# One more step of a scan's input products on GpSimd, and SiLU of z and the low rows of B and C in other slots

## The reference

```python
xz = x @ in_proj_w.T;  u, z = xz[..., :512], xz[..., 512:]
u = silu(causal_depthwise_conv4(u) + conv_b)
dt_lo, B, C = split(u @ x_proj_w.T, (64, 16, 16))
delta = softplus(dt_lo @ dt_proj_w.T + dt_proj_b);  A = -exp(A_log)
for t:                                   # 2048 positions
    h = exp(delta[t] * A) * h + (delta[t] * u[t]) * B[t]     # 512 x 16 states
    y[t] = h @ C[t]
y = (y + u * D_param) * silu(z)
x = layernorm(x + y @ out_proj_w.T)
h = silu(x @ w1 * s1) * (x @ w2 * s2)
h = gelu(h @ h1 * sh1);  h = gelu(h @ h2 * sh2)
x = layernorm(x + h @ w3 * s3)
```

## Time and profile before

| | us |
|---|---|
| median of 3 runs | 3013.3 (3012.48 to 3014.08) |
| the profiled execution | 3011.42 |
| its span, first to last instruction | 3009.6 |
| VectorE busy in the span | 2297.7 |
| ScalarE busy in the span | 2033.7 |
| GpSimd busy in the span | 1704.2 |
| TensorE matmuls busy in the span | 2720.0 |

### The profile page before, as it was taken

The page is one execution under the profiler, slowest core; times in us unless marked ns, Lnnn a source line. Parts: engine busy times, 40 slices in busy tenths (PEclk is TensorE's granted clock), DMA queues, the critical chain, the costliest instruction groups (busy, mean ns, idle before and its releaser), DMA issues. The chain is left out here.

```text
span 3009.6 us, 40984 instructions
## 1 busy us (share of the span) xinstructions
PE 2720.0 (90%) x11540; PEld 1619.3 (54%) x11540; DVE 2297.7 (76%) x2650; ACT 2033.7 (68%) x3600; POOL 1704.2 (57%) x839
## 2 busy tenths in 40 slices
PE   5798998998998998998998976999999999999997
PEld 2243443343443443443443432778888888888886
DVE  6999999999999999999999999144445444444452
ACT  3878877878878877877878877465544555555452
POOL 4899999999899989999999998100000000000000
PEclk8899999998999999999999987999999999999999
DMA  8565565565566565565565566632222222222210
GB/s 265 122 188 158 144 190 158 144 193 164 134 193 165 136 192 159 139 196 158 139 192 165 143 186 224 205 101 77 92 70 70 84 91 77 70 79 88 70 42 15
DMA packets 239646, 412.05 MB, mean 137 GB/s; under 512 B 23264, under 2 KB 63456, under 8 KB 239456
## 3 DMA queue, kind: packets, MB, share of 16 engines
q1 hardware_dynamic: 175680, 297.67, 36.6%
q10 hardware_dynamic: 63776, 112.22, 11.4%
HBM read 285.55 MB, written 124.26 MB: 136 GB/s over the span
## 5 line engine op out<-in xcount | busy, mean ns | idle before, releaser
L1284 DVE TENSOR_TENSOR_SCAN h<-bank,state,db 128x512 f32<-128x512 f32 x1024 | 1243.3, 1268 | 18.9 <-ACT bank L916 18.5
L1144 POOL TENSOR_TENSOR hc<-h,c_rows 128x1024 f32<-128x1024 f32 x512 | 1200.3, 2375 | 96.6 <-DVE h L1284 75.0
L916 ACT ACTIVATE bank<-d_bc,a_neg 128x512 f32<-128x512 f32 x1024 | 695.4, 685 | 251.8 <-DVE h L1284 240.6
L1625 ACT ACTIVATE hring<-s_bank,sc 128x512 f32<-128x512 f32 x248 | 170.4, 687 | 488.6 <-PE s_bank L1558 488.3
L1558 PE MATMUL s_bank<-mid,h_r 128*128 128x512 f32 x2048 | 468.7, 390 | 4.6 <-DVEq L1652 4.6
L1268 DVE TENSOR_TENSOR db<-bank,du_bc 128x2048 f32<-128x2048 f32 x192 | 435.7, 2269 | 2.5 <-issue 2.5
L1558 PEld LDWEIGHTS s_bank<-mid,h_r 128*128 128x128 f32 x2048 | 385.5, 188 | 85.6 <-ACTq L1596 5.0
L731 PE MATMUL bank<-x_t,w 128*128 128x512 f32 x1088 | 362.5, 461 | 60.7 <-ACT ab L993 53.9
L659 PE MATMUL bank<-hc,fold_w 128*32 128x512 f32 x2048 | 305.1, 671 | 23.0 <-DVE uz L1308 11.3
L731 PEld LDWEIGHTS bank<-x_t,w 128*128 128x128 f32 x1088 | 203.2, 200 | 216.6 <-ACT ab L993 101.0
L1155 POOL TENSOR_TENSOR db<-du_bc,b_row 128x2048 f32<-128x2048 f32 x64 | 291.4, 4553 | 16.0 <-DVE h L1284 15.9
(11 more groups left out here) (147 smaller groups left out, 3721.7 us busy)
## 6 DMA issues: line engine op xcount, KB each, us to landing
ab<-ab ACTq DMA_DIRECT2D x272, 256.0 KB, 3.8
du_bc<-du_rows SPq DMA_DIRECT2D x256, 256.0 KB, 4.7
d_bc<-d_rows SPq DMA_DIRECT2D x256, 256.0 KB, 7.7
s_abr<-ab SPq DMA_DIRECT2D x120, 512.0 KB, 3.7
w<-w ACTq DMA_DIRECT2D x136, 256.0 KB, 3.1
d_rows<-sp_r SPq DMA_DIRECT2D x64, 256.0 KB, 2.0
du_rows<-sp_w SPq DMA_DIRECT2D x64, 256.0 KB, 3.1
x<-res SPq DMA_DIRECT2D x17, 512.0 KB, 8.8
```

Of the source, the lines that this page charges most:

```text
L916: act.activation(decays[DECAY_BANK[g]][:], d_bc[c % 2][:, j, :], ACT.Exp, scale=a_neg[:, g:g + 1]).then_inc(decay, 1)
L1144: pool.tensor_tensor(hc[:, k % HCSTEPS, at:at + HG], h[:, H_SLOT[k], at:at + HG], c_rows[:, q, :].unsqueeze(1).broadcast_to([P, HG, NT]), ...
L1284: dve.tensor_tensor_scan(h[:, H_SLOT[k], j, :], decays[DECAY_BANK[g]][:], db[:, k % DBSTEPS, j, :], state[:, g:g + 1], ALU.mult, ALU.add). ...
L1625: act.activation(hring[c % RING][:], p_h[m % HBANKS][:], ACT.Gelu, scale=sc[:, 2 + layer, m:m + 1]).then_inc(gelu, 1)
```

## The change

- **A fifth step on GpSimd.** Step k = 10 of each tile (chunk 2, q = 2) joins steps 3, 7, 11 and 15: its product with B is made by GpSimd, not by VectorE. The semaphore counts of both engines' products follow (`dve_steps`, `pool_steps`).
- **Its row of B.** TensorE spreads it into the bank `p_dt` in slot 13 (with a wait for the softplus that used this bank), ScalarE copies it to the new buffer `b_row2` in slot 14, and TensorE no longer spreads it for VectorE. The transposes in slot 16, which use the same bank, wait for this copy.
- **The ring of w1/w2 buffers** has three places, not four; `b_row2` takes the fourth's.
- **SiLU of z** is in slot 60, not 63: the first slot of a step.
- **The low rows** are taken in slot 21, not 19.

```diff
+EXTRA_Q, EXTRA_C = 2, 2
+BY_POOL = [k % QN == QV or k == QN * EXTRA_C + EXTRA_Q for k in range(NK)]
+NPOOL = sum(BY_POOL)
+NDVE = NK - NPOOL
+def pool_steps(k):
+    return k // NK * NPOOL + sum(BY_POOL[:k % NK])
+def dve_steps(k):
+    return k - pool_steps(k)
...
+ROW2_SLOT = 13
...
-SILU_Z_SLOT = 63
+SILU_Z_SLOT = 60
...
-ABRING, W12RING = 3, 4
+ABRING, W12RING = 3, 3
...
+        b_row2 = sb("b_row2", [P, NT])
...
@@ SyncE, before the copies of du and d of chunk c
-                sp.wait_ge(db_dve, t.count(KI * QV, QV * (c - 1) + DVE0))
+                sp.wait_ge(db_dve, t.count(NDVE, dve_steps(QN * (c - 1)) + DVE0))
...
-                sp.wait_ge(db_pool, t.count(KI, c - 1 + POOL0))
+                sp.wait_ge(db_pool, t.count(NPOOL, pool_steps(QN * (c - 1)) + POOL0))
@@ TensorE
-                        if exists(now) and g // JC % QN < QV:
+                        if exists(now) and not BY_POOL[g // JC]:
                             spread_b(now, g // JC)
...
+                        if i == ROW2_SLOT:
+                            pe.wait_ge(sp_dve, t.count(2 * KI, 2 * KI))
+                            spread_rows(p_dt, t, EXTRA_Q, row2_mm)
                         ffn(t, i)
@@ TensorE, transposed(t, k, 0)
-                        pe.wait_ge(sp_dve, t.count(2 * KI, 2 * KI) if exists(t) else t.count(2 * KI, 0))
+                        pe.wait_ge(row2_sb, t.count(1, 1) if exists(t) else t.count(1, 0))
@@ ScalarE
+                        if i == ROW2_SLOT + 1:
+                            act.wait_ge(row2_mm, t.count(1, 1))
+                            act.wait_ge(db_pool, t.count(NPOOL, POOL0))
+                            act.activation(b_row2[:], p_dt[:], ACT.Copy).then_inc(row2_sb, 1)
                         ffn(t, i)
...
-                    load_w12(t.following(), m - KH)
+                    load_w12(t.following(), e // 2 % W12RING)
@@ GpSimd, times_b
+                c, q = divmod(k, QN)
+                row = b_row if q == QV else b_row2
                 pool.wait_ge(du_in[c % 2], t.count(2 * COPIES, COPIES * (c // 2 + 1)))
...
+                else:
+                    pool.wait_ge(row2_sb, t.count(1, 1))
                 pool.wait_ge(scanned, t.count(NG, JC * (k - DBSTEPS + 1) + SCANNED0))
...
-                        if exists(now) and g // JC % QN == QV:
+                        if exists(now) and BY_POOL[g // JC]:
                             times_b(now, g // JC)
@@ VectorE, scan
-                    if q < QV:
-                        dve.wait_ge(db_dve, t.count(KI * QV, QV * c + q + 1 + DVE0))
+                    if BY_POOL[k]:
+                        dve.wait_ge(db_pool, t.count(NPOOL, pool_steps(k) + 1 + POOL0))
                     else:
-                        dve.wait_ge(db_pool, t.count(KI, c + 1 + POOL0))
+                        dve.wait_ge(db_dve, t.count(NDVE, dve_steps(k) + 1 + DVE0))
@@ VectorE
-                        if exists(now) and g // JC % QN < QV:
+                        if exists(now) and not BY_POOL[g // JC]:
                             times_b(now, g // JC)
...
-                    if i == XD_SLOTS.stop + 1 and exists(nxt):
+                    if i == XD_SLOTS.stop + 3 and exists(nxt):
                         low_rows(nxt)
```

More of the change, by code:

```diff
@@ L313, in mamba_stage @@
         b_bc = sem("b_bc")
+        row2_mm, row2_sb = sem("row2_mm"), sem("row2_sb")
         decay = sem("decay")
@@ L517, in closing @@
                         sp.wait_ge(decay, t.count(NG, 3 * GC + DECAY0))
-                        sp.wait_ge(db_dve, t.count(KI * QV, 3 * QV + DVE0))
-                        sp.wait_ge(db_pool, t.count(KI, 3 + POOL0))
+                        sp.wait_ge(db_dve, t.count(NDVE, dve_steps(3 * QN) + DVE0))
+                        sp.wait_ge(db_pool, t.count(NPOOL, pool_steps(3 * QN) + POOL0))
                     elif m == 6:
@@ L642, in spread_b @@
                     pe.wait_ge(xd_lo, t.count(1, 1))
-                pe.wait_ge(db_dve, t.count(KI * QV, QV * c + q + DVE0))
+                pe.wait_ge(db_dve, t.count(NDVE, dve_steps(k) + DVE0))
                 spread_rows(p_b, t, q, b_bc)
@@ L712, in ffn_product @@
                 if which == 0:
-                    pe.wait_ge(w12_in[m % W12RING], t.count(16 * KH // W12RING, 16 * (m // W12RING + 1)))
+                    pe.wait_ge(w12_in[m % W12RING], t.count(16 * len(range(m % W12RING, KH, W12RING)), 16 * (m // W12RING + 1)))
                 before = product_before(t, e)
@@ L1148, in times_b @@
             def times_b(t, k):
-                c = k // QN
+                c, q = divmod(k, QN)
+                row = b_row if q == QV else b_row2
                 pool.wait_ge(du_in[c % 2], t.count(2 * COPIES, COPIES * (c // 2 + 1)))
-                if c == 0:
-                    pool.wait_ge(rows_sb, t.count(ROWS, 2))
+                if q == QV:
+                    if c == 0:
+                        pool.wait_ge(rows_sb, t.count(ROWS, 2))
+                else:
+                    pool.wait_ge(row2_sb, t.count(1, 1))
                 pool.wait_ge(scanned, t.count(NG, JC * (k - DBSTEPS + 1) + SCANNED0))
                 pool.tensor_tensor(db[:, k % DBSTEPS], du_bc[c % 2][:],
-                                   b_row[:].unsqueeze(1).broadcast_to([P, JC, NT]), ALU.mult).then_inc(db_pool, 1)
+                                   row[:].unsqueeze(1).broadcast_to([P, JC, NT]), ALU.mult).then_inc(db_pool, 1)
             def softplus(t, c, step):
@@ L1215, in round_piece @@
                     pool.wait_ge(first_lo, KH)
-                    pool.wait_ge(db_dve, LAST_ROW[-1].count(KI * QV, KI * QV + DVE0))
+                    pool.wait_ge(db_dve, LAST_ROW[-1].count(NDVE, NDVE + DVE0))
                     pool.wait_ge(folded, LAST_ROW[-1].count(NK, NK + FOLDED0))
@@ L1263, in times_b @@
                 c, q = divmod(k, QN)
-                dve.wait_ge(b_bc, t.count(KI * QV, QV * c + q + 1))
+                dve.wait_ge(b_bc, t.count(NDVE, dve_steps(k) + 1))
                 if q == 0:
@@ L1336, in closing @@
                             dve.wait_ge(decay, t.count(NG, NG + DECAY0))
-                            dve.wait_ge(db_pool, t.count(KI, KI + POOL0))
+                            dve.wait_ge(db_pool, t.count(NPOOL, NPOOL + POOL0))
                         dve.tensor_tensor(first_parts[1][:, m, :], first_abr[m][:, 1, :],
```

2 lines of the change are left out of this document (1 added, 1 removed).

## The result

The change makes the kernel slower: 3070.08 us (median of 4 runs, 3067.75 to 3075.55) against 3013.5 us before (median of 4), ratio 1.0193 [1.0181, 1.0205], +56.6 us. The forecast was 3055 us in 3033 to 3077: the sign and the range held, the size was 15 us short.

The account below looks back on a forecast made before the run. VectorE was taken to bound the first stage, with GpSimd becoming late at step 11. GpSimd's longer list, +47, and SiLU, -5, gave +42 us on 3011.4, 3053.4; with the runs' median 1.9 higher, 3055 us, range 3033 to 3077.

Parts of the forecast that it names:

- What bounds the kernel: First stage: VectorE sets the 112.4 us tile period, waiting 1.5 us per tile; GpSimd's margin at step 11 is 1.36 us.
- Part 1: Step 10's product leaving VectorE saves it 2.18 us per tile; GpSimd takes 4.51 us for the same.
- Part 2: GpSimd's list from step 7's product makes step 11 start later, 2.95 us per tile, +47 us (+38 to +56).
- Part 3: SiLU of z in slot 60 cuts VectorE's waits for decays by 0.3 us per tile: -5 us (-18 to +8).
- Part 4: Low rows' slot, ScalarE's copy into `b_row2`, TensorE's row spreading, three weight buffers and SyncE's queue together cost nothing.
- From step 11 to the next step 7 nothing gives this time back: VectorE's order there is as before, so the 2.83 us by which step 11 starts later in the tile read stays lost.
- rival 2: The loss comes back: after a stall VectorE's later waits for ScalarE and TensorE vanish, 3042 us; chance 0.05.
- rival 1: GpSimd isn't late at the new product, VectorE keeps 2.9 us per tile, -46 us: 2967 us; chance 0.07.
- Rival 3: Shared SBUF port: the new product holds up scans beside it, 4.5 us more per tile, 3127 us; chance 0.03.
- Rival 4: Lost margin spreads: products of steps 15, 3 and 7 late by up to 1 us each, 3071 to 3103; chance 0.1.

Follow-up runs that it names:

- Groups 3 and 4: Kernel before with two or three split products: 3012.57, 3012.39 us; SiLU in slot 60 except at the loop's end: 3013.31; three split, less TensorE work: 2970.51.
- split products: Against the kernel before, GpSimd makes one group of four of the products of steps 5 and 13 (then also 1), VectorE the rest: 3012.57 (3012.39) us.
- group 1: Kernels taking the change apart: SiLU alone 3014.07 us, all but fifth product and row 3015.44, fifth product alone 3071.1, all but the product itself 3015.98.

## Why the prediction came out as it did

**What bounds the kernel** was half right. VectorE sets the pace before step 7's product, and GpSimd's margin at step 11 was the right thing to look at. But the prediction took VectorE's 1.5 us of waits per tile for small, local things. Groups 3 and 4 show, for the kernels with split products, a second bound close behind, TensorE's list by way of ScalarE: work taken off VectorE comes back there as waits. That the 1.5 us of the kernel before are already its edge is likely by this, but wasn't tested.

**Part 1, VectorE's saving.** As forecast: line 1300 has 176 products, 11 per tile. None of the saving was to be kept, and none was.

**Part 2, GpSimd's sum.** It held to the instruction: 36.96 us measured in the tile shown, 36.95 forecast; the distance between the products of steps 7 and 11 is 844.84 - 812.67 = 32.17, 32.3 forecast. Over all 16 tiles the first VectorE product behind step 11's first scan starts 38.15 us after step 7's product, in every tile 37.97 to 38.29, where before it was 35.00 (33.98 to 35.54). So the step costs 3.15 us per tile, forecast 2.95: +50.4 against +47. In the tile shown VectorE waits 3.11 us at step 11 (forecast 3.9) and 0.70 + 0.53 + 0.56 = 1.8 around step 10 (forecast 1.4), of which only the last is for GpSimd; the 0.70 is a step earlier, for a decay, for which the product that left had been the cover. Over all tiles the forecast was 32 waits for GpSimd of 85 us. The scans of steps 10 and 11 that start within 0.3 us of the end of GpSimd's product waited 60 us in 30 cases, 49.3 at step 11 and 10.6 at step 10. All idle time of VectorE between step 8's second scan and step 11's first is 83.5 us, before it was 9.1. So the stall has about the forecast size, but a quarter of it is spent on ScalarE and TensorE on the way, while GpSimd's list runs on. Reading it off the `POOL db` line would have failed.

**Part 3, SiLU.** The gain isn't there: -5 forecast, +1.9 measured alone with an interval that holds zero, and the change without it (the fifth product alone) is 1 us from the change. The wait behind SiLU did fall (all waits for decays from 14.4 to 8.4 us in 13 tiles, a little more than forecast), but at the loop's end VectorE's jump came out of hiding, and where this was avoided the waits behind the softplus grew. The step that failed is that a wait of VectorE for ScalarE was counted as gained when the instruction ahead of the decays moved.

**Part 4, the rest.** "Nothing" was nearly right: +3.3 us for SiLU, low rows and ring together, +3.8 with the row's spreading and copy, both with SiLU's 2 in them.

**"From step 11 to the next step 7 nothing gives this time back".** Right in that no time came back, rival 2 didn't happen. But some was added: the stretch from step 12's product to the next step 8's took 84.29 us on the mean, 83.59 before, +0.70 per tile. It is the one term that the sum didn't have. In the tile shown it lies behind a softplus (VectorE, step 13):

```profile
883.88 0.70 DVE L1323 SCALAR_TENSOR_TENSOR bank<-sp_w,bank 128x512 f32<-128x512 f32 x1 [0.95 <-ACT bank L912]
```

and TensorE just before it, with the matmuls of the softplus (line 636):

```profile
871.74 1.23 PE L750 MATMUL bank<-x_t,w 128*128 128x512 f32 x4 [1.86 <-ACT ab L1016]
...
877.49 2.07 PE L636 MATMUL bank<-xd,w_dt 64*128 64x512 f32 x2
879.49 2.07 PE L750 MATMUL bank<-x_t,w 128*128 128x512 f32 x4
```

The busy time by window, columns as in the earlier trace rows, for a stretch behind that idle time and the one after it:

```profile
874.00:883.00 9.00, 9.00 (x21) 2.64 (x17) 8.75 (x7) 5.86 (x12) 9.00 (x4) 0.50 0.59 197
884.00:900.00 16.00, 14.51 (x56) 6.62 (x53) 16.00 (x13) 12.03 (x24) 14.04 (x7) 1.00 0.64 196
```

Behind an idle time of 1.86 us the granted clock is 0.50, the lower level (1.2 GHz). The softplus' two matmuls take 2.07 us, where at the full clock a pair took 1.12 in the kernel before, and what hangs on them comes late. VectorE's waits behind the softplus were 9.9 us in 400 to 1850 us and are 16.2, and the mean granted clock was 0.953 and is 0.937. It is tempting to blame the stall at step 11 for this. But the kernel of group 1 that has no fifth product, and no stall, shows nearly the same:

```profile
DVE bank L1314 <- ACT bank L908: 16.0, 35, 1.0
```

Its stretch is 84.17 us, and that of the kernel with the fifth product alone 83.92, with the row alone 83.80, with SiLU alone 83.63. So at most a part of the 0.70 is the stall's. Of these, the two with the longest stretches were also profiled in executions that took 5.5 and 4.2 us more than their medians, some 0.3 us per tile. What adds this time stays open.

For the profiled execution the sum then reads 50.4 + 15 x 0.70 = 61 us of 64, against 42. The difference of 19 is 3.4 from the size of part 2, 5 from SiLU's missing gain and 10.5 from what was added; the last 3 us of the 64 lie outside the 16 tiles. By the medians it is shorter: of the 56.6 us, 50.4 are part 2 and 3.8 all that the change has besides the product (group 1). Against the forecast of 42 that is 3.4 more for part 2, 8.8 for the other parts, where -5 was forecast, and 2.4 without a place.

**The rivals.** GpSimd was late in all tiles, so rival 1 (2967 us) falls. Rival 3, the shared port, would have shown as scans or products at another pace; they had the same means, and the time that GpSimd's instruction takes reappears as the length of its own list. The Trainium skill (Perfetto Trace Analysis, Optimizing Scalar/DVE Operations) warns that moving work between the two engines "might not help". It didn't, but by the trace the reason isn't the port that it names. Rival 4 had the margin spread to the products of steps 15, 3 and 7. The measured 3070 is near its low end (3071), but not for its reason: in the traces what was added is a wait for ScalarE and TensorE, and GpSimd still waits for VectorE ahead of the products of steps 15 and 7 (0.94 and 1.88 us in the tile shown). So its mechanism wasn't seen.

## What to carry to other kernels

Before work moves to an engine that has idle time, add up that engine's list between the two points that the move lies between, and hold the sum against the other engine's; 6.7 us of idle time per tile didn't help, because at most 0.7 us of it lay in that stretch. A wait of the busiest engine for a second one may be a third one's, passed on: look at what the second waits for before counting it as gained. And if removing work from the bound moves nothing, make the list of the next suspect lighter, even if that leaves part of the result out, to see whether it holds the time.

## What the runs showed of the hardware

- At the jump back to the start of a loop an engine got no new instruction for 2.8 to 4.0 us (VectorE, by the trace's branch and the next instruction behind it; 0.10 us where the branch wasn't taken). It cost VectorE nothing where a product and three scans were already lined up (2.9 us, hidden), and 2.7 to 3.1 us where its last scan ahead of the jump had to wait for a decay. ScalarE's cost it 2.30 us with nothing to run, and 0 where a block of 4.5 us stood right ahead of it.
- GpSimd's product of a quarter of the size took 1.26 to 1.33 us where the whole takes 4.55, and of half the size 2.35; VectorE's of three quarters took 1.73 us, the whole 2.27. Worked out from these, an estimate: each further piece costs some 0.15 us on either engine.
- TensorE behind an idle time of 1.86 us: four matmuls of 128x512 in 2.07 us, elsewhere in 1.2; of the two clock levels (1.2 and 2.4 GHz) it was at the lower one there, by the granted clock of 0.50 in the windows shown above. The mean granted clock of the whole run was 0.953 before and 0.937 after.
- The name in the bracket of a wait was the wrong engine's in several of the 3 us waits at step 11. The end of GpSimd's product, 0.09 to 0.21 us before the scan's start, told the releaser. At the loop's end the bracket named `POOL hc` or `issue` for a wait that was VectorE's own jump.
